# One score step of each attention slot stands further back in the order of the work

## What is computed

```python
xn = _layernorm(x)
q, k, v = split(xn @ w_attn)              # 16 heads of 8
scores = q @ k.T / sqrt(8) + causal - log1p(decay[h] * log1p(dist))
y = softmax(scores) @ v
x = x + y @ w_proj + moe(xn)              # top 2 of 8 experts, silu, gates
```

## Time and profile before

| | |
|---|---|
| time, median of 3 runs (lowest to highest) | 531.16 us (529.22 to 532.96) |
| the profiled execution's own time | 531.62 us |
| its span in the trace | 529.8 us |
| PE busy | 482.3 us, 91% of the span |
| DVE busy | 360.5 us, 68% |
| granted TensorE clock, mean | 0.974 |

### The profile page before, as it was taken

One profiled execution on the slowest core, in us unless ns is written; L12 is line 12 of the kernel. 1 busy time (PEld: TensorE's weight loads), 2 busy tenths in 40 slices (PEclk: granted clock), 3 DMA queues, 4 the chain that ended last, 5 costly groups with the idle time before them and its releaser, 6 DMA issues.

```text
span 529.8 us, 13373 instructions
## 1 busy us (share of the span) xinstructions
PE 482.3 (91%) x4316; PEld 351.6 (66%) x4316; DVE 360.5 (68%) x1406; ACT 335.6 (63%) x600; POOL 338.4 (64%) x566
## 2 busy tenths in 40 slices
PE   7767999989999999999999999999999999999920
PEld 6545566555565665665565565666999999999910
DVE  7595997988988878888878878872433333333326
ACT  3578878878878878878878878776232333333300
POOL 2873555556888878876878888970454555555524
PEclk9988999999999999999999999999999999999975
DMA  6566591570460451450460451355466677666449
GB/s 179 168 232 207 156 219 47 157 214 8 136 185 23 135 173 36 137 164 23 136 181 27 137 165 50 107 171 141 121 201 190 209 215 207 207 183 207 131 166 319
DMA packets 71826, 80.38 MB, mean 152 GB/s; under 512 B 8638, under 2 KB 52672, under 8 KB 71760
## 3 DMA queue, kind: packets, MB, share of 16 engines
q1 hardware_dynamic: 67440, 71.06, 45.8%
q0 software_dynamic: 4320, 8.47, 4.5%
HBM read 48.11 MB, written 31.84 MB: 151 GB/s over the span
## 4 chain that ended last, share of the span: by engine, by line
PE 72%; DVE 18%; POOL 3%; DMA 2%; ACT 2%; issue 2%; SPq 0%; DVEq 0%; ACTq 0%; POOLq 0%
PE psT L1291 22%; PE psO L1309 13%; PE ps L1336 12%; DVE scores L1121 12%; PE psT L1363 12%; PE ps L1266 7%; PE psM L1250 2%; POOL xn_all L734 2%; DVE x_all L535 2%; PE ps L1327 1%; PE psM L1320 1%; DMA probs<-picked_dram 1%; POOL rstd L727 1%; ACT probs L884 1%; DMA decay_in<-decay_raw 1%
## 5 line engine op out<-in xcount | busy, mean ns | idle before, releaser
L1121 DVE CUSTOM_DVE_ANT_0 scores<-ps,wdist 128x256 f32<-128x256 f32 (+3 forms) x512 | 218.6, 486 | 28.1 <-PE ps L1266 25.4
L765 POOL TENSOR_SCALAR scores<-scores,row_max 128x256 f32<-128x256 f32 (+2 forms) x384 | 177.5, 477 | 62.9 <-DVE row_max L1121 61.6
L884 ACT ACTIVATE probs<-psT 128x512 f32<-128x512 f32 x320 | 173.7, 594 | 54.8 <-PE psT L1291 54.4
L1291 PE MATMUL psT<-ident,scores 128*128 128x128 f32 x1280 | 177.2, 281 | 3.4 <-ACT probs L884 2.8
L1291 PEld LDWEIGHTS psT<-ident,scores 128*128 128x128 f32 x1280 | 137.6, 141 | 63.7 <-issue 37.5
L783 POOL DMA_INDIRECT picked_dram<-scores,row_ring x71 | 69.7, 982 | 80.6 <-DVE scores L1173 79.1
L893 ACT ACTIVATE scores<-ps 128x512 f32<-128x512 f32 x71 | 42.4, 597 | 95.1 <-PE ps L1336 95.1
L846 ACT ACTIVATE scores<-scores,row_max 128x512 f32<-128x512 f32 x128 | 84.8, 714 | 0.0
L1309 PE MATMUL psO<-probs,values 128*32 128x512 f32 (+3 forms) x1024 | 82.0, 438 | 0.0
L1336 PE MATMUL ps<-scores,wdist 128*128 128x128 f32 x568 | 75.3, 276 | 0.8 <-DVE scores L1161 0.8
L1363 PE MATMUL psT<-wdist,scores 128*128 x568 | 75.3, 276 | 0.6 <-ACT scores L893 0.6
(11 more groups left out here) (140 smaller groups left out, 277.4 us busy)
## 6 DMA issues: line engine op xcount, KB each, us to landing
wdist<-w1t SPq DMA_DIRECT2D x71, 256.0 KB, 3.2
k_rows<-k_dram SPq DMA_DIRECT2D x64, 96.0 KB, 2.8
q_rows<-q_dram SPq DMA_DIRECT2D x64, 96.0 KB, 2.6
row_ring<-rows_dram SPq DMA_DIRECT2D x71, 65.0 KB, 3.0
probs<-picked_dram SPq DMA_DIRECT2D x8, 512.0 KB, 6.8
rows_dram<-row_ring SPq DMA_DIRECT2D x7, 585.0 KB, 5.8
k_dram<-k_parts SPq DMA_DIRECT2D x7, 384.0 KB, 2.3
q_dram<-q_parts SPq DMA_DIRECT2D x7, 384.0 KB, 2.6
```

What stands on the lines that cost most here:

```text
L765: last = nc.gpsimd.tensor_scalar(part, part, -1.0, row_max[:, r, tile, quad:quad + 1], ALU.mult, ALU.add)
L884: nc.scalar.activation(probs[:, at.ring(2), w, :], psT[:, w % 2], ACT.Exp, scale=-1.0).then_inc(exp_ready, 1)
L1121: last = nc.vector.tensor_tensor_reduce(out=scores[:, r, u, col:col + n], in0=bank[:, col:col + n], in1=wdist[:, at.g * QUADS + quad, SEQ ...
L1291: last = nc.tensor.transpose(psT[:, w % 2, place * P:(place + 1) * P], scores[:, at.ring(2), u, col + key * P:col + (key + 1) * P], ident[:])
```

## The change

Step P1 1 is taken out of the opening run of each slot but the first and put behind the first two value products, PV 0 and PV 1. With it moves everything that hangs on it: its products on PE, its pieces on DVE, its subtraction on POOL, and the routing pieces of index 1 in slots 2 to 4 (`R2`, `R5`, and `CT`, the count products of slot 4, with its copy on ACT).

```diff
     p1(0)
-    p1(1)
+    if n == 0:
+        p1(1)
     step("TE", n - 1, NGROUP, 0, 2)
...
     step("SA", n, NGROUP, (0, 1))
     step("PV", n - 2, NGROUP, 0)
     step("PV", n - 2, NGROUP, 1)
+    if n > 0:
+        p1(1)
     per_batch("KR", -3)
     per_batch("QR", -2)
     step("TE", n - 1, NGROUP, 2, 4)
```

## The result

| | before | after |
|---|---|---|
| time, median of 12 runs on one chip (lowest to highest) | 530.04 us (528.77 to 532.96) | 534.15 us (533.34 to 536.4) |
| ratio, 95% interval | | 1.0077 [1.0059, 1.0095] |
| the profiled execution's own time | 531.62 us | 534.38 us |
| its span | 529.8 us | 532.5 us |

A forecast was written before the change was run, and what follows sets the result against it. PE was taken to set the pace of the slots; 17 x 0.24 - 6 x 0.13 = +3.3 us, plus +0.3 us in slots 2 to 8, gave +3.6 us on 531.16 us: 534.8 us, range 529 to 540.5 us.

The forecast's parts named there:

- P1 0 to the first transposes: Opening run on PE: falls from 0.81 to 0.35 us with P1 0 alone, removing 0.46 us a slot.
- P1 1 in its new place: On PE between PV 1 and TE 2: from its load to the first transpose it takes 0.33 us.
- passage from the value products to P1 1: On PE, PV into a score step: taken to cost the same as PV into transposes, adding nothing.
- rival 2: On PE, the passage from PV to a score step is dear: 0.17 us in 30 slots, +5.1 us, 539.9 us; chance 0.12.
- wait of P1 3: On PE, P1 3 waits 0.37 us for P1 1's two banks in slots without PJ, none with PJ.
- the slot with PJ: Six of slots 9 to 31: -0.46 + 0.33 = -0.13 us each, as P1 3 doesn't wait.
- way of 1.95 us: From P1 4's load over DVE to the waiting load of P1 1; against 1.58 us of PE work between P1 1 and P1 3.
- rival 3: Opening wait goes and no new one comes, slots 2 to 31: -7.6 us, 523.6 us; chance 0.07.
- the first (DVE late to P1 1): DVE over 0.26 us later at P1 1 than counted; P1 3's wait doubles: +6.3 us, 541.1 us; chance 0.17.
- moving YT costs nothing: On DVE in slot 22, YT now ahead of P1 1 ends with 0.4 us to spare.
- Slots 2 to 8: Early slots, DVE 90% busy: between a 4.6 us gain and a +1.3 us price, taken as +0.3 us.
- held by the prologue: Slot 1: its time is set by the prologue, so no term was counted for it.

The follow-up runs named there:

- first experiment: Against the changed kernel, P1 1 moved to right behind TE 0 and 1, ahead of KA or QA and the value products: 527.81 us, ratio to before 0.9946.
- second: Against the changed kernel, P1 1 put between the two value products PV 0 and PV 1: 530.7 us, ratio to before 1.0006.
- third experiment: Against the changed kernel, P1 1 left in place and P1 3 moved from behind P1 2 to behind TE 4 and 5: 531.66 us, ratio to before 1.0019.
- last experiment: Against the changed kernel, YT put behind P1 1 on DVE again: one execution, 537.58 us.

## Why the prediction was right

The forecast was 534.8 us, +3.6 us and a ratio of 1.0068; measured were 534.15 us, +4.1 us and 1.0077 [1.0059, 1.0095]. Its steps, in a slot without PJ:

| step | predicted | measured, slot 22 |
|---|---|---|
| P1 0 to the first transposes | 0.35 us | 259.53 to 259.88: 0.35 |
| removed by that | 0.46 | 0.81 - 0.35 = 0.46 |
| P1 1 in its new place | 0.33 | 263.44 to 263.76: 0.32 |
| passage from the value products to P1 1, beyond that to transposes | 0 (rival 2: +0.17) | 1.65 - 1.64 = +0.01 |
| wait of P1 3 | 0.37 | 0.60 - 0.23 = 0.37 |
| TE 0 to the value products | no change | 1.91 - 1.89 = +0.02 |
| the slot | +0.24 | 10.47 - 10.20 = +0.27 |
| the slot with PJ | -0.13 | 10.12 - 10.23 = -0.11 |

The removed wait and the new one came out to the hundredth. The way of 1.95 us from load over DVE to load, read at P1 4 and P1 1, held at the new place: 263.43 to 265.38 is 1.95 us again. That 0.37 us is a difference of two sums of nearly the same size, my case for rival 3, did no harm: both are made of measured starts that repeat in every slot. And less than 1% could be told from no change after all: 12 executions of each kernel gave an interval of 1.0059 to 1.0095.

The runs put a price on a change of shape: 0.19 us for one more passage in and out beside the transposes (first experiment), 0.14 inside the value products (second). They show the times alone, and not what goes on in the array at a passage. The change itself pays less, and pays it inside the forecast's terms. The way out of the value products costs the same into P1 1 as into transposes (the table's +0.01). But a step that stands alone takes 0.31 or 0.32 us up to the transposes, and one with another score step behind it 0.23; so parting P1 0 and P1 1 costs 0.08 or 0.09 us, which the forecast had in its 0.35 and 0.33. In the third experiment, where P1 3 is parted from P1 2, the price is 0.10 us.

Of the rivals, the first (DVE late to P1 1) fell in slots 9 to 31, but for one. In slot 22 DVE was done with YT and waited for P1 1; I had counted 0.4 us to spare:

```profile
262.70 0.70 DVE L1153 STREAM_TRANSPOSE yt<-y_q 128x512 f32<-128x512 f32 x1
263.86 0.56 DVE L1124 CUSTOM_DVE_ANT_0 scores<-ps,wdist 128x384 f32<-128x384 f32 x1 [0.46 <-PE ps L1269]
```

The one is slot 30, which has YT but no QA, so P1 1 comes sooner while YT is still there:

```profile
343.14 0.70 DVE L1153 STREAM_TRANSPOSE yt<-y_q 128x512 f32<-128x512 f32 x1
343.77 0.51 DVE L1124 CUSTOM_DVE_ANT_0 scores<-ps,wdist 128x384 f32<-128x384 f32 x1
```

There is no idle time between the two rows, P1 3 waits 0.23 us longer, and the slot lost 0.50 us. The prediction's sentence "moving YT costs nothing" was worked out for slots with both YT and QA and for slots with neither, and left this third kind out. The last experiment showed the price by taking it away (+0.28). Rival 2 fell by the 1.65 us; its 0.17 us, the idle ahead of a load of score products behind transposes (256.43 and 257.89 in the earlier trace rows), did not come on top behind the value products, where the load of P1 1 has the same 0.62 us of idle that the transposes' load had there before (at 262.23 us); the dearest passages (0.14 and 0.19 us) were those where P1 1 parts products that would otherwise share a shape, as in the first two experiments. Rival 3 was not what this change does, but it is close to what P1 1 ahead of the value products does: 30 slots nearly without the wait, and -3.9 us.

Three terms were mis-sized. The sum over slots 9 to 31 was +3.3 us by the forecast and +4.01 in the trace: 15 slots without PJ came out 0.03 us dearer each (0.52 in all), slot 30 0.26 and the six with PJ 0.13 together, while slot 12, whose old wait the forecast had not counted, came out 0.20 cheaper. Slots 2 to 8 cost +0.74 us where I took +0.3 out of -4.6 to +1.3. And slot 1, "held by the prologue", was put at nothing, but is 1.58 us shorter in the trace, 0.47 of it because TE 0 no longer waits behind P1 1 there. So the whole came out nearer than its parts, and that is in part luck: slots 2 to 31 took 4.75 us more in the traces against the forecast's 3.6, while the medians differ by 4.11; what lies outside these slots, slot 1 above all, made up for it.

In slots 2 to 8 the differences go from -0.69 (slot 7, with PJ) to +0.90 us (slot 2). In five of the seven P1 3 waits longer than 0.37 us, from 0.48 (slots 2 and 5) to 1.00 (slot 6), and in return the old waits ahead of P1 1 go (in slot 6 it started 1.11 us behind P1 0 before, not 0.49). In slot 2, P1 1 and the routing pieces that moved along with it come just ahead of QR on DVE now, so QM on ACT, and the exponentials behind it, come late: QM starts 2.21 us behind P1 2, before it was 0.64, and TE 6 then waits 0.53 us on PE.

```profile
59.74 0.60 ACT L867 ACTIVATE q_parts<-psM 128x512 bf16<-128x512 f32 x1 [1.46 <-DVE psM L971]
```

In slot 6 P1 1 starts on PE at 99.56 us, and DVE takes it up 1.09 us later, straight behind YT, instead of 0.42 us later as in slot 22; P1 3 then starts 1.24 us behind P1 2. DVE, then PE:

```profile
100.01 0.71 DVE L1153 STREAM_TRANSPOSE yt<-y_q 128x512 f32<-128x512 f32 x1
100.65 0.52 DVE L1124 CUSTOM_DVE_ANT_0 scores<-ps,wdist 128x384 f32<-128x384 f32 x1
```

```profile
99.56 0.39 PE L1269 MATMUL ps<-k_rows,q_rows 48*128 48x384 bf16 x4
...
100.90 0.39 PE L1269 MATMUL ps<-k_rows,q_rows 48*128 48x256 bf16 x4
102.14 0.39 PE L1269 MATMUL ps<-k_rows,q_rows 48*128 48x512 bf16 x2 [0.84 <-DVE row_max L1124]
```

What was not tried: a kernel with more than four score banks, which should take the wait away without moving a step; that is my estimate, from the order of the steps alone.

## What to carry to other kernels

A step with two pairs of buffers has two neighbours in the order: the one whose buffers it waits for, and the one that waits for its own. Before moving it, measure the whole way from its load over the consumer back to the next load (1.95 us here) and lay against it the work that will stand in between, on both sides and for every kind of slot. Look for the next wait behind the one that goes, too: in the third experiment it was TE 4's for the exponentials. And of the places that give the same cover, take the one where the array changes its shape anyway: here that was worth 0.19 us in each slot with KA or QA.

## What the runs showed of the hardware

- A passage between two shapes of the array has no single price in these runs. From the value products (four strips of 32 columns) into score products (two halves of 48 rows) it is the same as into transposes (1.65 us in slot 22 of the kernel after and 1.64 in that of the kernel before, from start to start), but one put between transposes and products of the same shape cost 0.19 us (first experiment), one in the middle of the value products 0.14 (second), and a score step parted from the step that it shared a passage with 0.10 (third).
- The idle time of a weight load that names a releaser need not be a wait: 0.62 us named DVE in slot 22 and nothing in slot 23, at the same place, with the same length.
- A true wait is not read off an idle time either. At P1 3 of slot 22 the load sat idle for 0.49 us and PE for 0.21, since a matmul still in flight counts as busy; the starts, compared with a slot without the wait, say 0.37 (0.60 against 0.23).
